# Bidirectional Mamba scan stage: reverse drives made by TensorE from turned du and diagonal blocks of b, reverse states read by GpSimd

## The reference, cut to what matters

```python
u     = silu(conv1d(in_proj_x(seq)));  z = in_proj_z(seq)
dt,B,C = x_proj(u);  delta = softplus(dt_proj(dt) + dt_b);  A = -exp(A_log)
def step(h, inp):                       # h: one number per channel and state
    u_t, d_t, B_t, C_t = inp
    dA = jnp.exp(d_t[..., None] * A)                       # the decay
    h  = dA * h + (d_t * u_t)[..., None] * B_t[:, None, :] # the drive is du * b
    return h, jnp.einsum('bdn,bn->bd', h, C_t)             # the read
y = scan(step) + u * D;  out = out_proj(y * silu(z))
result = 0.5 * (mamba(seq) + flip(mamba(flip(seq))))       # forward and reverse
```

## Time and profile before

| | us |
|---|---|
| median of 3 runs | 27,766.99 (27,764.99 to 27,772.45) |
| the profiled execution, whole | 27,768.75 |
| its span, first to last instruction | 27,767.2 |
| busy: POOL / DVE / PE / ACT | 25,520.0 / 25,925.0 / 18,178.2 / 16,996.5 |
| mean granted TensorE clock | 0.81 |

### The profile page before, as it was taken

How to read it: one execution, slowest core, us unless ns; L and a number is a source line. 1 busy time by engine, 2 the same in 40 slices (tenths; PEclk the granted TensorE clock), 3 DMA queues, 4 the chain that set the end, 5 groups by cost and what they waited for, 6 DMA issues and landing times. The chain is left out here.

```text
span 27767.2 us, 284715 instructions
## 1 busy us (share of the span) xinstructions
PE 18178.2 (65%) x62778; PEld 5277.9 (19%) x62778; DVE 25925.0 (93%) x24107; ACT 16996.5 (61%) x23653; POOL 25520.0 (92%) x11268
## 2 busy tenths in 40 slices
PE   6666666666666666666666666666666666666572
PEld 1111111111111111111111111111111111111120
DVE  8999999999999999999999999999999999999321
ACT  6666666666666666666666666666666666665232
POOL 8999999999999999999999999999999999999000
PEclk8888888888888888888888888888888888887786
DMA  5555555555555555555555555555555555555967
GB/s 189 202 200 202 200 201 199 200 199 199 200 202 200 202 199 201 200 200 200 199 201 201 201 200 200 201 200 200 200 198 202 200 202 201 201 200 183 188 130 180
DMA packets 1914996, 5473.26 MB, mean 197 GB/s; under 512 B 214002, under 2 KB 642818, under 8 KB 1901458
## 3 DMA queue, kind: packets, MB, share of 16 engines
q1 hardware_dynamic: 1912968, 5451.83, 57.9%
HBM read 4644.92 MB, written 805.60 MB: 196 GB/s over the span
## 5 line engine op out<-in xcount | busy, mean ns | idle before, releaser
L796 POOL TENSOR_TENSOR drive<-du_rep,b_rep 128x1024 f32<-128x1024 f32 x8192 | 19201.4, 2389 | 114.5 <-DMA b_rep<-bc_spread 75.1
L729 DVE TENSOR_TENSOR_SCAN decay<-decay,drive 128x512 f32<-128x512 f32 x10752 | 12658.3, 1218 | 132.9 <-issue 54.6
L599 ACT ACTIVATE decay<-delta_rep,a_neg 128x1016 f32<-128x1016 f32 x8192 | 8999.1, 1106 | 598.4 <-DMA delta_rep<-delta_spread 593.6
L453 PE MATMUL y_bank<-read,sel_f 128*32 128x512 f32 x32768 | 5510.3, 805 | 2702.1 <-DVE gated L751 1798.0
L742 DVE TENSOR_TENSOR read<-decay,c_rep 128x1024 f32<-128x1024 f32 (+1 forms) x5632 | 6528.0, 1159 | 0.0
L729 DVE TENSOR_TENSOR_SCAN state<-decay,drive 128x512 f32<-128x512 f32 x5120 | 6203.7, 1212 | 83.8 <-ACT decay L599 81.3
L809 POOL TENSOR_TENSOR read<-state,c_rep 128x1024 f32<-128x1024 f32 x2560 | 6099.0, 2382 | 0.0
L595 ACT COPY decay<-zeros 128x8 f32<-128x8 f32 x5632 | 946.8, 168 | 6807.3 <-DVE read L742 6626.3
L430 PE MATMUL p_bank<-e_one,sel_f 128*128 128x512 f32 x2048 | 1563.5, 854 | 2769.4 <-ACT e_one L580 2487.2
L407 PE MATMUL p_bank<-xt,taps 128*128 128x512 f32 x4096 | 2069.2, 627 | 950.1 <-ACT u L538 492.0
L453 PEld LDWEIGHTS y_bank<-read,sel_f 128*32 128x32 f32 x32768 | 1076.1, 131 | 6474.4 <-issue 4959.4
(11 more groups left out here) (109 smaller groups left out, 14419.8 us busy)
## 6 DMA issues: line engine op xcount, KB each, us to landing
du_rep<-du_spread SPq DMA_DIRECT2D x2048, 512.0 KB, 6.4
delta_rep<-delta_spread SPq DMA_DIRECT2D x2048, 512.0 KB, 6.2
b_rep<-bc_spread SPq DMA_DIRECT2D x2048, 512.0 KB, 7.7
c_rep<-bc_spread SPq DMA_DIRECT2D x2048, 512.0 KB, 4.1
du_spread<-e_log SPq DMA_DIRECT2D x512, 512.0 KB, 2.7
delta_spread<-e_one SPq DMA_DIRECT2D x512, 512.0 KB, 3.6
xt<-in_xs SPq DMA_DIRECT2D x1024, 128.0 KB, 3.4
bc_spread<-bc SPq DMA_DIRECT2D x1024, 64.0 KB, 1.6
```

Of the source, the lines that this page charges most:

```text
L453: mm = nc.tensor.matmul(y_bank[32 * j:32 * j + 32, :], gather, read[:, (ROW * m + j) % READ_RING, px(d)], start=(m == 0 and d == FWD), sto ...
L599: nc.scalar.activation(inner(place[:, :]), inner(delta_rep[:, j, :]), ACT.Exp, scale=a_neg[s][:, ROW * j + m:ROW * j + m + 1]).then_inc(s_ ...
L729: nc.vector.tensor_tensor_scan(to[:, ::step], decay[place_of(turn, h, q)][:, px(d)][:, ::step], drive[:, q % DRIVE_RING, px(d)][:, ::step] ...
L796: nc.gpsimd.tensor_tensor(drive[:, q % DRIVE_RING, :], du_rep[h][:, j, :], b_rep[:, m, :], ALU.mult).then_inc(s_drive, 1)
```

## The change

- The reverse direction leaves the pairs. A unit now has 16 slots. Even slots 2f are forward: 8 operations that hold two channel blocks j side by side (1024 columns of one state group m). Odd slots 2r+1 are reverse: 8 operations with 128 rows = 4 state groups g by 32 channels, and 1024 columns = 2 sequences by 4 states m by 128 steps.
- Reverse drives are made by PE into the PSUM places. du is turned (`turn_du`) so that 64 time steps lie on partitions, and serves as the stationary operand; b is turned too (`project_b_cols`), stored to a DRAM image of zeros, and loaded so that `b_diag` holds, for each step, the 16 states on the diagonal and zeros elsewhere. The product is du*b exactly, step by step. `b_diag` is read with the state outside and the step inside, 16 elements (64 bytes) from one step to the next. A drive is one matmul of 16 columns and 16 of 256 columns, on tiles of 64 rows by 32 columns of the array.
- Reverse decays go to SBUF (`decay_r`, 16 activations of 508 elements); forward decays go to the places, two activations of 508 each.
- DVE scans 1024 columns in one instruction. A reverse scan reads the decay from SBUF and the drive from PSUM and writes `read_r`; POOL multiplies that in place by `c_r`, all eight.
- POOL makes 8 forward drives, and reads 2 forward states in a unit of h=0 and 3 in one of h=1 (`F_BY_POOL`); DVE reads the other 6 and 5, each right behind its own scan.
- The ring of three places now serves forward decays and reverse drives in turn.
- SP issues 40 transfers per unit where it issued 23; `b_diag` is 2 MB per unit in pieces of 4 KB, and the pieces of the other loads are 1 or 2 KB instead of 4 KB.
- Once, at the start, the image is zeroed (8 stores).

```diff
-BY_POOL = (1, 4, 7, 10, 13)
-DRIVE_RING, READ_RING, STATE_RING = 4, 8, 2
+F_OPS = R_OPS = 8
+SLOTS = F_OPS + R_OPS
+WINDOW = 64
+F_BY_POOL = ((1, 5), (1, 4, 7))
+PLACES, DRIVE_RING, F_RING, R_RING = 3, 3, 4, 6
+DRIVE_AHEAD = 2
...
+STEPS = [Step("bt", REV, 1, 0, 1), Step("ds", FWD, 1, 1, 2), Step("ds", REV, 1, 3, 4),
+         Step("tr", REV, 1, 7, 7), Step("bc", 0, 1, 7, 8),
+         Step("x", FWD, 2, 8, 9), Step("x", REV, 2, 8, 9), Step("z", 0, 1, 9, 10),
+         Step("dt", FWD, 2, 10, 11), Step("dt", REV, 2, 11, 12), Step("out", 0, -1, 13, 14)]
...
+            def load_diag(h, pair, r):
+
+                image = spill["image"][h]
+                src = bass.AP(image.tensor, image.offset + (2 * pair * P + WINDOW * r) * IMAGE_ROW
+                              + (WINDOW - 1) * NS,
+                              [[IMAGE_ROW - NS, WINDOW], [P * IMAGE_ROW, 2], [1, WINDOW * NS]])
...
+            def make_drive(U, i, h, turn, r):
+
+                to = place[place_of(turn, h, 2 * r + 1)]
+                ti, th, f = before_f(i, h, r)
+                if not (isinstance(ti, int) and ti < 0):
+                    if f in F_BY_POOL[th]:
+                        pe.wait_ge(s_state, F_OPS * U + r)
+                    else:
+                        pe.wait_ge(s_read_v, read_by_vector(ti, th, f) + 1)
...
+                nc.tensor.matmul(to[0:32, 0:NS], du_cols[h][:, 2 * pair, 32 * j:32 * j + 32],
+                                 b_diag[:, pair, 0, 0:NS], start=True, stop=True, tile_position=(0, 0),
+                                 skip_group_check=True)
+                for half in range(2):
+                    for row in range(2):
+                        rows = slice(WINDOW * row, WINDOW * row + WINDOW)
+                        diag = b_diag[rows, pair, half, :].rearrange("p (t n) -> p n t", n=NS)
+                        part = to[:, px(row)].rearrange("p (m t) -> p m t", m=ROW)
+                        part = part[:, :, WINDOW * half:WINDOW * half + WINDOW]
+                        for g in range(4):
+                            mm = nc.tensor.matmul(part[32 * g:32 * g + 32, :, :],
+                                                  du_cols[h][rows, 2 * pair + half, 32 * j:32 * j + 32],
+                                                  diag[:, 4 * g:4 * g + 4, :], start=True, stop=True,
+                                                  tile_position=(WINDOW * row, 32 * g),
+                                                  skip_group_check=True)
+                mm.then_inc(s_drive_r, 1)
...
+                nc.vector.tensor_tensor_scan(read_r[:, r_slot(turn, h, r), :][:, ::-1], r_decay(r),
+                                             place[place_of(turn, h, 2 * r + 1)][:, ::-1], 0.0,
+                                             ALU.mult, ALU.add).then_inc(s_state_r, 1)
...
+                    for f in range(F_OPS):
+                        if f > 0:
+                            read_r_state(U, h, f - 1, turn)
```

More of the change, by code:

```diff
@@ L452, in sum_row, with sum_r @@
+            def sum_r(U, h, turn, pair):
+                pe.wait_ge(s_read_r, R_OPS * U + ROW * pair + ROW)
+                part = slice(2 * SIDE * pair, 2 * SIDE * pair + 2 * SIDE)
+                for m in range(ROW):
                     for j in range(ROW):
-                        mm = nc.tensor.matmul(y_bank[32 * j:32 * j + 32, :], gather,
-                                              read[:, (ROW * m + j) % READ_RING, px(d)],
-                                              start=(m == 0 and d == FWD), stop=(m == 3 and d == REV),
+                        slot = read_r[:, r_slot(turn, h, ROW * pair + j), :]
+                        slot = slot.rearrange("p (s m t) -> p s m t", s=2, m=ROW)
+                        mm = nc.tensor.matmul(y_bank[32 * j:32 * j + 32, part], gather[1], slot[:, :, m, :],
+                                              start=False, stop=(m == 3 and pair == 1),
@@ L1534 @@
         arrays[f"out_t_{s}"] = w["out_w"].T
-        arrays[f"a_log_{s}"] = w["A_log"].reshape(ROW, 32, ROW, 4).transpose(1, 3, 0, 2).reshape(P, PAIRS)
+        a = w["A_log"].reshape(ROW, 32, NS)
+        forward = a.reshape(ROW, 32, ROW, 4).transpose(1, 3, 0, 2).reshape(P, NS)
+        order = np.array([[state_of(m, g) for m in range(ROW)] for g in range(4)])
+        reverse = a[:, :, order].transpose(2, 1, 0, 3).reshape(P, NS)
+        arrays[f"a_log_{s}"] = np.concatenate([forward, reverse], 1)
         arrays[f"cols_{s}"] = np.stack([w["conv_b"], w["dt_b"], w["D"]], 1)
```

574 lines of the change are left out of this document (367 added, 207 removed).

## The result

The changed kernel takes 29,864.87 us (median of 4 runs, 29,802.51 to 29,894.35) against 27,769.72 for the kernel before in the same session: a ratio of 1.0752, 95% interval [1.0732, 1.0771]. It is 7.5% slower, where 26,300 us was forecast, and outside the range. The profiled span is 29,892.5 us.

The account below looks back on a forecast made before the run. DVE was to bound at 43.9 us per unit, PE the same at 44.0 and 3.1 us late at slot 11: 47.0 x 512 + 2,207 + 30 = 26,301, so 26,300 us. Forecast case 25,700 to 27,500 (0.42); range 24,700 to 29,000 us.

Parts of the forecast that it names:

- POOL 42.8, DVE 43.9 us: Work per unit after the change on the two engines: POOL 42.8 us, DVE 43.9 us with reads waiting for scans.
- The flat price: POOL's operations with repeated operands or runs of 128 cost the same 2.31 us as flat ones; upper end 0.1 more each.
- ACT 36.5: ACT's work per unit, up from 32.1 to 36.5 us, hidden by DVE's 43.9 with 7 us of slack.
- D = 1.6: One reverse drive on PE: small product 0.58 us, then 32 records on eight tiles at once 1.0; lower end 1.2.
- PE 41.4 at the full clock, 0.94: PE's work per unit, 28.6 us plus eight drives 12.8; at a granted clock of 0.94 it is 44.0 us.
- Slot 11, 3.1 us late: From slot 9's drive to slot 11's, PE needs 13.2 us against DVE's 10.1, so slot 11 is 3.1 late per unit.
- Elsewhere I take nothing: Other slot pairs: PE late by up to 1.5 us for once, with light pairs on both sides, so no loss counted.
- Transfers, "I take no wait": DMA share of the engines 60% by bytes, 106% by packets (some 5,900 per unit); bytes taken as nearer, no wait.
- Rival (b), the strided read: b_diag's 64-byte step halves the matmul rate, a drive takes 2.45 us, PE fills: 28,450 us; chance 0.25 with all slow-drive reasons.
- the sign of (b): The drives' matmuls busy 15 us or more per unit, against near 8 us for the forecast.
- The sum: 43.9 us of DVE plus 3.1 of lateness per unit, 512 units, plus 2,207 and 30 us: 26,301 us.
- the forecast of 47.0: Time per unit in us: DVE's 43.9 plus 3.1 late at slot 11.

Follow-up runs that it names:

- the best kernel: Changed kernel with first two forward delta loads ahead of b and c, b columns taken in slot 0, four states inside, u times D in slot 6: 27,666 us.
- the attempt to remove the second: The 27,666 us kernel with bc computed in slot 3 instead of 7 and its store ahead of the loads of du and delta_r: 29,134 us.

## Why the prediction was wrong

- **POOL 42.8, DVE 43.9 us.** Right: 43.3 busy on POOL; on DVE 44.0 busy and 0.6 in which a read waits for its own scan. The flat price held for both new patterns.
- **ACT 36.5.** 35.2, near enough. That ACT stands in a fixed order, and that each product it waits for holds the decays behind it, was not weighed: this is how a wait of PE or of a load reaches DVE.
- **D = 1.6.** 2.05. The small product was taken too dear (0.58 from a pair that stands behind 7.18 us of waiting at a granted clock of 0.50; 0.16 here) and the wide ones too cheap (1.0, they take 1.9 with the step). Eight tiles do run at once: 32 records in 4 x 0.43 us and a tail, and 3.63 us with four tiles.
- **PE 41.4 at the full clock, 0.94.** 46.2 us busy at 0.92. D alone would have added 8 x 0.45 = 3.6 us at the full clock. By busy time times clock, 46.2 x 0.92 = 42.5, the other work was taken some 2.5 us too dear; that is an estimate.
- **Slot 11, 3.1 us late.** The right place, and 4.6 to 4.9 us. Of the 1.3 us that the stretch is longer, two drives are 0.9.
- **"Elsewhere I take nothing".** This is the step that failed. 3.0 us for the first du product and 1.4 for the decay behind delta_f are 4.4 of the 7.2 us by which the unit is longer than forecast; the wait for drives is 1.8 above its 3.1, DVE's own work and its waits for itself 0.7. The dearest pair that was looked at, slots 3 and 4 with 3.6 us of softplus, holds the second product, and that one takes 3.7. The first, in slots 1 and 2, takes 6.7, nearly all at the lower clock, and starts 1.1 us late, since it waits for ACT to take the b columns.
- **Transfers, "I take no wait".** This failed with it. The packets were foreseen (6,147 per unit, 9.70 MB), the share of the engines is 69% and not 60. The loads were judged by their bytes and packets alone; what counted was their place in the queue behind the store of bc. ACT waits 2.2 us per unit for delta_f and POOL 2.1 for b. A smaller b_diag, or its load at another place, was not tried.
- **Rival (b), the strided read.** Its mechanism is shown (603 against 428 ns) and its price isn't: PE was to fill up and give 28,450 us. The drives are busy 15.5 us per unit, which was named as the sign of (b), and yet the step by itself is not why the kernel is slow. With the read in line the time is 29,925 us. It may have a part together with other edits, as in the best kernel.
- **The sum.** All terms were added as if an engine that finishes early gains what it finishes early. A drive made longer by 1.7 us costs 3,378 us, half of 8 x 1.7 x 512; one made shorter by 0.85 gives nothing by itself.

Shown by single edits: the queue's order is worth 1,017 us, ACT's late take of the b columns 944. The gap ahead of slot 9's drive has no edit of its own; what is known is that the three products behind it take 1.4 us per unit more with the states inside than with the step. The two edits, the faster read and u times D in slot 6 together bring the kernel from 29,865 to 27,666 us, 49.9 us per unit. That is 2.9 us above the forecast of 47.0, which had allowed for 3.1 us of waits. DVE waits there 1.6 us for du, 1.5 for POOL's drives behind the load of b, 1.2 for PE's drives and 0.5 for forward decays; the attempt to remove the second failed, since the loads of b then landed late. Many of the variants sit at 52.0 to 52.2 or 54.1 to 54.5 us per unit, whichever wait they remove. I take this to mean that several rings of about equal length run through the same engines; I did not trace every ring, and which one binds in each variant stays open.

## What to carry to other kernels

Before removing a wait in a kernel of engines with fixed orders and short rings (here three places), list for each engine what stands behind its own next wait, the DMA queue included: a load that waits for a store holds every load behind it, and a small store issued behind large loads lands late. Price a matmul by the gap in front of it as well: on an engine that is not the bound, time saved can be given back by the work that follows at 1.2 GHz. Useful work that stands in the gap is worth 509 us in the best kernel, but the same move cost 213 us in the changed one, where PE waited only 0.43 us at that place. And when an experiment leaves work out, look in its trace at how long the rest takes: here one matmul of 16 took as long as all of them with the faster read, so the run priced the gap and not the drive.

## What the runs showed of the hardware

- At 2.4 GHz a moving operand of 4-byte elements read 64 bytes apart costs twice: 0.43 us per group of 256 columns, 0.215 when four neighbours (16 bytes) are inside. At 1.2 GHz the step costs nothing: 1.96 us per drive both ways. Steps between 4 and 64 bytes were not tried.
- Eight tiles of 64 rows by 32 columns run at once: the 32 records of a drive take 1.93 us on eight and 3.63 on four.
- Writing the result to PSUM 512 bytes apart costs nothing: 428 ns a record, as with neighbours.
- Two matmul records of 16 columns take 0.16 us of PE when others follow at once; the pair of the earlier trace rows, with 2 columns and a wait in front, is shown with 0.58.
- Less work on PE can make the kernel slower: with drives of the same length, 1.2 us, the kernel that leaves 15 of 16 matmuls out has a granted mean of 0.82 against 0.88, and takes 702 us more.
- The granted mean over a stretch does not tell what a stretch costs: the best kernel has 0.89, the changed one 0.92. Which instructions run at the lower level does.
- What is issued ahead of a small store sets when it lands: 64 KB in 6.7 us (median) right behind eight loads of 256 KB, in 2.7 us ahead of them. The same holds for loads: those of b land in 6.4 us in the changed kernel and in 12.9 us where SyncE issues them sooner behind the others.
